# Fixed roles for the PSUM pairs, tanh from gelu's table set, and a new order around the trip's seam

## The reference

```
xn = layernorm(x)
x  = x + mixed_attention(xn) + ternary_ffn(xn)           # layer 0
xn = layernorm(x)
x  = x + hyperbolic_attention(xn) + gated_ffn(xn)        # layer 1

mixed_attention: 16 heads of 8, causal window of 128, plus 4 latent heads over 64 pooled tokens, mixed by a sigmoid gate
hyperbolic_attention: u -> (cosh|u|, sinh|u| u/|u|);  z = max(-<q,k>, 1+1e-7);  scores = -arccosh(z)^2/sqrt(8); causal softmax
gated_ffn: h = silu(x w1 * s1) * (x w2 * s2)              # 128 -> 512
           h = gelu(h h1 * g1);  h = gelu(h h2 * g2);  y = h w3 * s3
```

## Time and profile before

| what | us |
|---|---|
| median of 3 runs | 3143.15 |
| the profiled execution | 3142.96 |
| its span, first to last instruction | 3141.2 |
| PE busy | 2314.6 (74%) |
| PE weight loads, beside PE | 1750.7 (56%) |
| ACT busy | 1760.9 (56%) |
| DVE busy | 1725.3 (55%) |
| POOL busy | 1211.9 (39%) |

### The profile page before, as it was taken

The page is one execution under the profiler, slowest core; times in us unless marked ns, Lnnn a source line. Parts: engine busy times, 40 slices in busy tenths (PEclk is TensorE's granted clock), DMA queues, the critical chain, the costliest instruction groups (busy, mean ns, idle before and its releaser), DMA issues.

```text
span 3141.2 us, 51003 instructions
## 1 busy us (share of the span) xinstructions
PE 2314.6 (74%) x17440; PEld 1750.7 (56%) x17440; DVE 1725.3 (55%) x3470; ACT 1760.9 (56%) x2510; POOL 1211.9 (39%) x1274
## 2 busy tenths in 40 slices
PE   0567877778777778777777787777887777877776
PEld 0345655656555556555565565565665555655555
DVE  7355555655555565655555655565555556555551
ACT  4125655565655555555555565556465556555566
POOL 2224443443443443343343343344244344334332
PEclk9979888989888889988889888898898898988888
DMA  4222212211211211211221221221121121121110
GB/s 127 57 56 56 56 32 55 57 40 47 57 42 42 57 47 40 57 48 37 55 57 30 57 55 30 55 57 41 46 57 42 42 57 46 41 57 49 36 29 4
DMA packets 298755, 153.12 MB, mean 49 GB/s; under 512 B 13360, under 2 KB 295248, under 8 KB 298704
## 3 DMA queue, kind: packets, MB, share of 16 engines
q1 hardware_dynamic: 298704, 152.45, 19.0%
HBM read 81.11 MB, written 71.30 MB: 49 GB/s over the span
## 4 chain that ended last, share of the span: by engine, by line
PE 36%; issue 22%; DVE 19%; ACT 14%; POOL 8%; DMA 0%; DVEq 0%; ACTq 0%; POOLq 0%; SPq 0%
PE pu L1635 6%; PE pu L1454 6%; PE pu L1425 4%; POOL zs L1081 3%; PE pu L1434 3%; DVE nmax L665 3%; DVE zc L829 2%; ACT zc L1274 2%; PE pm L1646 2%; ACT hid L1269 2%; DVE resid L642 2%; PE pu L1468 2%; PE pm L1510 2%; ACT zs L1273 1%; ACT L1269 1%
## 5 line engine op out<-in xcount | busy, mean ns | idle before, releaser
L1425 PE MATMUL pu<-k_st,q_st 128*128 128x128 bf16 (+1 forms) x2048 | 318.4, 265 | 244.6 <-DVE nmax L665 223.6
L1057 POOL TENSOR_SCALAR_AFFINE_SELECT prob<-prob 128x512 f32<-128x512 f32 x128 | 81.5, 637 | 844.1 <-ACT prob L1222 841.9
L1070 POOL TENSOR_TENSOR zs<-zc,zs 128x1024 f32<-128x1024 f32 x160 | 379.8, 2391 | 65.8 <-ACT zc L1274 65.8
L665 DVE TENSOR_REDUCE nmax<-pu 128x4 f32<-128x1024 f32 (+1 forms) x192 | 234.6, 1222 | 307.3 <-PE pu L1434 307.3
L665 DVE TENSOR_REDUCE zmin<-pu 128x4 f32<-128x1024 f32 (+1 forms) x192 | 234.6, 1222 | 268.2 <-PE pu L1434 160.6
L1425 PEld LDWEIGHTS pu<-k_st,q_st 128*128 128x128 bf16 x2048 | 186.5, 106 | 336.7 <-DVE nmax L665 242.3
L1001 POOL TENSOR_TENSOR rs<-ve,mhalf 128x2 f32<-128x2 f32 x64 | 45.7, 714 | 665.1 <-DVE ve L631 658.3
L1635 PE MATMUL pu<-hid,h1t 128*128 128x256 f32 x1024 | 275.2, 417 | 0.0
L1222 ACT ACTIVATE prob<-pu 128x1024 f32<-128x1024 f32 x160 | 163.7, 1024 | 159.3 <-PE pu L1454 159.2
L1635 PE MATMUL pu<-hid,h2t 128*128 128x256 f32 x1024 | 247.2, 385 | 0.0
L829 DVE TENSOR_SCALAR zc<-pu 128x1024 f32<-128x1024 f32 x192 | 232.8, 1212 | 0.0
(11 more groups left out here) (267 smaller groups left out, 5715.7 us busy)
## 6 DMA issues: line engine op xcount, KB each, us to landing
scr<-parts SPq DMA_DIRECT2D x256, 192.0 KB, 2.4
q_st<-scr SPq DMA_DIRECT2D x128, 256.0 KB, 4.1
k_st<-scr SPq DMA_DIRECT2D x64, 512.0 KB, 5.4
scr<-parts SPq DMA_DIRECT2D x128, 128.0 KB, 2.4
x<-in_L_attn_x SPq DMA_DIRECT2D x32, 128.0 KB, 2.1
out<-xold SPq DMA_DIRECT2D x32, 128.0 KB, 1.8
h1t<-in_h1t SPq DMA_DIRECT2D x1, 1024.0 KB, 7.5
h2t<-in_h2t SPq DMA_DIRECT2D x1, 1024.0 KB, 9.8
```

What stands on the lines that cost most here:

```text
L665: return V.tensor_reduce(out=dst, in_=u.ap.rearrange("p (h k) -> p h k", k=width), axis=AX_X, op=op, negate=negate)
L1070: G.tensor_tensor(zs[:, c], zc[:, c], zs[:, c], ALU.add).then_inc(sum_done[1].sem, 1)
L1425: PE.matmul(bank[:, s * width:(s + 1) * width], q_st[layer][:, h // 2, h % 2, q], k_st[layer][:, h // 2, 0:width], start=(s == 0), stop=False)
```

## The change

Five things are done together.

1. **Pairs.** `unit0` holds only min and max units. `av` takes exp0, exp1, exp5, the two attentions, sub0 to sub3, sub5 and f1_0; `unit1` takes exp4, exp2, exp3, f3, sub4, f2 and f1_2.
2. **Silu by tanh.** silu(a) b = (tanh(a/2) + 1) a b / 2. s1 is halved at the start, and s1 s2 is folded into `h1t`, once. ACT computes tanh, in gelu's table set, ahead of the gelus; DVE has two products per half (`gate_values`, `gated`), each over 128x512, in place of two of 128x256.
3. **Embedding** on DVE ahead of the last two min units; PE takes the last min unit behind the last `sub`.
4. **Minima at the seam.** `min0` is the first thing in a trip on PE and DVE.
5. **The order of the rest** on PE, ACT and DVE is written anew: feed3 and feed2 chunks are spread among the square transposes, attention and max units; on ACT one root pair instead of two stands ahead of `operands1`.

The diff, cut to its core; first the pairs, the weights' folding and the products:

```diff
-        UNIT_USES = [uses(M, [EXP[0]]) + uses(L, MIN) + uses(F, MAX) + uses(M, ["f1_0"]),
-                     uses(M, [EXP[4], EXP[2], EXP[5], EXP[3]]) + uses(E, ["f3"] + SUB[1::2]) + uses(L, ["f2"]) + uses(M, ["f1_2"])]
-        AV_USES = uses(M, [EXP[1], "av0", "avT0"]) + uses(E, SUB[0::2] + ["av1", "avT1"])
+        UNIT_USES = [uses(L, MIN) + uses(F, MAX),
+                     uses(M, [EXP[4], EXP[2], EXP[3]]) + uses(E, ["f3", SUB[4]]) + uses(L, ["f2"]) + uses(M, ["f1_2"])]
+        AV_USES = uses(M, [EXP[0], EXP[1], EXP[5], "av0", "avT0"]) + uses(E, SUB[:4] + SUB[5:] + ["av1", "avT1"]) + uses(M, ["f1_0"])
...
+            pre(V.tensor_scalar(s1[:], s1[:], 0.5, None, ALU.mult))
+            pre(V.tensor_tensor(s2[:], s2[:], s1[:], ALU.mult))
+            pre(V.tensor_tensor(h1t[:], h1t[:], bc(s2[:].unsqueeze(2), [P, HC, HID]), ALU.mult))
...
+                a = u.ap.rearrange("p (n k t) -> p n k t", n=2, k=2)[:, :, 0, :]
+                h = hid1[:, chunks[0]:chunks[-1] + 1, :]
+                link(V.scalar_tensor_tensor(h, h, 1.0, a, ALU.add, ALU.mult))
...
+                V.tensor_tensor(h, b, h, ALU.mult).then_inc(u.free, 1)
```

On DVE, in its iteration:

```diff
+                minima(0)
                 if e:
                     spikes(e, link[E])
                     least_squares(e)
-                minima(0)
-                if m:
-                    latent_out(run)
-                minima(1)
                 if f:
                     pool_tokens(run, f, link[F])
+                minima(1)
+                if m:
+                    latent_out(run)
...
                     sinh_series(m, link[M])
-                minima(5)
+                    embedding(m, link[M])
+                minima(4, 5)
...
+                    gate_values(run, m, "f1_0", (0, 1), link[M])
                 if f:
                     shift_lo(run, "mT", 0, f)
                 if m:
-                    gated(run, m, "f1_0", (0, 1))
-                    gated(run, m, "f1_2", (2, 3))
+                    gated(run, "f1_0", (0, 1))
+                    gate_values(run, m, "f1_2", (2, 3), link[M])
+                    gated(run, "f1_2", (2, 3))
```

On ACT:

```diff
                     root(run, l, 0)
-                    root(run, l, 1)
                 if m:
                     operands1(run, m)
                 if l:
+                    root(run, l, 1)
...
+                S.preload_act_table_set(GELU)
+                if m:
+                    tanh(run, m, "f1_0", (0, 1))
                 if f:
                     shift_part(run, "mT", 0)
+                if m:
+                    tanh(run, m, "f1_2", (2, 3))
...
-                    S.preload_act_table_set(SILU)
-                    silu(run, m, "f1_0", (0, 1))
-                    silu(run, m, "f1_2", (2, 3))
```

On PE:

```diff
-                transposes(2)
-                if m:
-                    project1(run)
-                transposes(3)
-                minima(5)
-                transposes(4)
+                feed3(2)
+                if m:
+                    project1(run)
+                feed3(3)
+                transposes(2)
+                minima(4)
+                transposes(3, 4)
...
                 transposes(5)
+                minima(5)
+                feed2(0)
...
                 attend1(0, 1)
+                feed2(1)
                 maxima(1)
                 attend1(2, 3)
-                feed2(0)
+                feed2(2)
                 maxima(2)
-                feed2(1)
+                feed2(3)
                 maxima(3)
```

More of the change, by code:

```diff
@@ L197, in wait_drained @@
         eng.wait_ge(self.free, self.count + 2)
-DVE_LINKS = {"norm": 2, "first": 1, "middle": 27, "last": 1, "end": 6}
+DVE_LINKS = {"norm": 2, "first": 1, "middle": 29, "last": 1, "end": 6}
 def bc(ap, shape):
@@ L841, in least_squares, with gate_values, gated @@
                 V.scalar_tensor_tensor(nmax[1][:], z3, -1.0, z3, ALU.mult, ALU.mult).then_inc(squares_ready.sem, 1)
-            def gated(run, m, name, chunks):
+            def gate_values(run, m, name, chunks, link):
                 u = unit(run, name)
                 dve.wait_ge(sil_ready.sem, sil_ready.at(m, 1 if name == "f1_0" else 2))
[L847 to L850, removed]
+                a = u.ap.rearrange("p (n k t) -> p n k t", n=2, k=2)[:, :, 0, :]
+                h = hid1[:, chunks[0]:chunks[-1] + 1, :]
+                link(V.scalar_tensor_tensor(h, h, 1.0, a, ALU.add, ALU.mult))
+            def gated(run, name, chunks):
+                u = unit(run, name)
+                b = u.ap.rearrange("p (n k t) -> p n k t", n=2, k=2)[:, :, 1, :]
+                h = hid1[:, chunks[0]:chunks[-1] + 1, :]
+                V.tensor_tensor(h, b, h, ALU.mult).then_inc(u.free, 1)
                 if name == "f1_2":
@@ L1248, in operands1, with tanh @@
                 hi_part(1, run.first, m)
-            def silu(run, m, name, chunks):
+            def tanh(run, m, name, chunks):
                 u = unit(run, name)
@@ L1256, in silu @@
                     o = n * BANK
-                    last = S.activation(hid1[:, c, :], u.ap[:, o:o + T], ACT.Silu, scale=s1[:, c:c + 1])
+                    last = S.activation(hid1[:, c, :], u.ap[:, o:o + T], ACT.Tanh, scale=s1[:, c:c + 1])
                 last.then_inc(sil_ready.sem, 1)
@@ L1372, in iteration @@
                 if e:
+                    weights1(run, 2)
+                    hidden(unit(run, "f3"), range(HC), hid3, g2)
                     for n in range(3, UNITS):
@@ L1384, in iteration @@
                 if l:
-                    for n in range(3, UNITS):
-                        root(run, l, n)
+                    root(run, l, 3)
+                    root(run, l, 4)
+                    hidden(unit(run, "f2"), range(HC), hid2, g1)
+                    root(run, l, 5)
                     minima_root(l)
-                    hidden(unit(run, "f2"), range(HC), hid2, g1)
+                if e:
+                    u = misc(run, "yT")
+                    copied(u, out_t[:], u.ap[:, 0:T])
+                S.preload_act_table_set(GELU)
+                if m:
+                    tanh(run, m, "f1_0", (0, 1))
                 if f:
                     shift_part(run, "mT", 0)
+                if m:
+                    tanh(run, m, "f1_2", (2, 3))
                 if e:
@@ L1673, in iteration @@
                 attend1 = lambda *groups: attend(avuse(run, "av1"), 1, groups) if e else None
-                if m:
-                    misc(run.before(), "mT").wait_drained(pe)
-                weights(0, 4, 1)
-                if m:
-                    latent_scores_t(run)
                 if l:
@@ L1682, in iteration @@
                 minima(0)
-                weights(2)
+                if m:
+                    misc(run.before(), "mT").wait_drained(pe)
+                weights(0, 4)
+                if m:
+                    latent_scores_t(run)
+                weights(1, 2)
                 if f:
@@ L1701, in iteration @@
                 attend0(0, 1)
+                if m:
+                    latent_back(run)
                 if f:
@@ L1704, in iteration @@
                 minima(2)
+                attend0(2, 3)
+                if m:
+                    latent_project(run)
                 if e:
@@ L1708, in iteration @@
                 if m:
-                    latent_back(run)
-                attend0(2, 3)
-                if m:
-                    latent_project(run)
-                feed3(1)
-                if m:
                     attended_t(avuse(run, "avT0"), 0)
-                minima(3)
                 if f:
@@ L1719, in iteration @@
                     project_latent(run, f)
-                feed3(2)
                 transposes(0)
@@ L1723, in iteration @@
                     mixed_t(run, m)
-                feed3(3)
+                minima(3)
                 if m:
                     layer0_out(run, m)
-                minima(4)
+                feed3(1)
                 transposes(1)
```

41 lines of the change are left out of this document (16 added, 25 removed).

## The result

The changed kernel takes **2667.59 us** (median of 4 runs, 2661.49 to 2670.63) against 3142.81 for the one before, measured in turn with it: a ratio of **0.8486**, 95% interval 0.847 to 0.8502. The forecast was 2577 with a range of 2464 to 2707, so the sign is as forecast and the gain is 475 us in place of 566. PE is busy for 83% of the span, DVE 69%, ACT 64%, POOL 45%, and the mean granted clock is 0.955.

The account below looks back on a forecast made before the run. PE and its waits bound the kernel: of a 92.5 us trip, 65.3 is full-clock work. With 8.0 of waits the trip becomes 73.3, saving 19.2, 557 over 29 trips plus 9 at the ends: 3143 − 566 = 2577 us, range 2464 to 2707.

Parts of the forecast that it names:

- the ends: Start and partial trips (1, 2, 32, 33): +3 us for folding s1 and s2, −12 for waits, a gain of 9.
- the forecast's own signs: Logarithm every 73 us, no PE wait over 2, clock 0.97 or more, three loads, exp some 8.5 after last max unit.
- the four waits: PE's waits before a max unit (7.3), embedding's transposes (6.1), output projection (2.4), next first scores (1.8): 17.6 us, all to go.
- the 7.3: PE's wait before the third max unit, its reduction queued behind DVE's split; earlier handover and PE fillers would remove it.
- PE's work: PE's work in one trip at full clock: 70.76 − 5.5 = 65.3 us.
- The seam: Between trips: next exp 8.5 us after the last max unit, before 12.6; waits of 2.4 and 1.8 go.
- The table load: ACT's table loads taken at 1.28 us each, without the skill's drain (2.66 in all), which would add 78 us.
- The embedding: Moved 2.5 us earlier in DVE's chain; PE reaches it 0.9 us after it is ready, and the 6.1 wait goes.
- Three priced new waits: New PE waits per trip: yffn 1.5, third square transposes 1.3, split before third max unit 1.05; 3.9 us.
- Rivals 2, 3 and 4: Seam waits for k transfer: 2681, chance 0.15; av pair becomes bound: 3273, 0.04; tanh needs its own load, nothing gained: 0.01.
- the six small ones as today, 4.1: The trip's six other PE waits, longest 1.0, carried over into the new trip's sum at 4.1 us.
- Rival 1: PE's clock keeps falling behind short waits: 5.5 us stay in the trip, +160, 2737 us; chance 0.20.

Follow-up runs that it names:

- e5: Changed kernel with the embedding alone put back behind the last min units on DVE and PE: 2835.89 us.
- e10: As e9, and ACT again takes two root pairs ahead of the handover to the split: 2699.97 us.
- e3: Changed kernel with both edits, that of e1 and that of e2: 2488.29 us.
- e8: e3, and DVE takes the second min unit and the copy of lo ahead of the token sums: 2451.56 us.
- e4: Changed kernel with tanh alone undone: silu from its own table, the old four products, a fourth table load per trip: 2719.21 us.
- e2: Changed kernel with POOL's square of unit 1 moved ahead of its split and that of unit 3 behind the residual: 2571.36 us.
- e1: Changed kernel with the head norm's two-SBUF-operand product (L658) removed, the spike mask entering as a maximum with a PSUM operand: 2574.16 us.
- e7: Changed kernel with fifteen overwritten matmuls added per trip, eight in PE's wait before gr, seven before the last max unit: 2615.87 us.
- e9: Changed kernel with PE's feed2 chunks put back to their old places among the max units: 2683.96 us.

## Why the prediction was right, and where it was short

**Size of the miss.** 91 us on the medians, 93 on the profiled execution: the trips gave 455.6 in place of 557 (101 short), the ends 17 in place of 9. Per trip that is 77.51 against 73.3, of which 0.7 comes from the trip that was read (92.50 where the mean of 29 is 93.22) and 3.5 is the miss. That the ends gave 8 more than forecast is luck: their −12 was not worked out, and no run looked into it. Of the forecast's own signs only the three loads came out in full: trips of 77.5 for 73, a longest wait of 2.07 for 2, a clock of 0.96 and 0.98 for 0.97, the exp at 9.8 for 8.5.

**What held.**
- *The bound and the four waits.* PE and its waits were the right ledger: all four went, and the longest wait that is left is 2.1. The walk's reason for the 7.3 is borne out in part: e5 and e10 show that its early handover and chunks, and the early embedding with the split free of the sums, each keep most of it away.
- *PE's work.* 65.3 at 2.4 GHz; 64.94 and 65.32 in e3 and e8, at clock 1.00.
- *The seam.* Exp at 8.5 forecast, 9.8 measured. The first two tanh ended at 4.5 where 3.05 had been taken, since PE's two projections ahead of them ran in the stretch at clock 0.50. Both waits went all the same.
- *The table load* at 1.28: the load at 1424.03 ends at 1425.31, the logarithm starts at 1425.32. One load more put the exp 1.3 us later in e4. The Trainium skill, "ScalarE: Activation LUTs", What ACT_TABLE_LOAD costs, has 2.66 per switch, by estimate 77 us in 29 trips; neither the rows nor e4 (52 us in all) bear it out here.
- *The embedding.* It ended at 1391.15 (DVE, L812), and its transposes started on PE at 1391.98: 0.8 behind it, 0.9 forecast.
- *Three priced new waits.* yffn 1.2 (lo_t) for 1.5, third sub 1.0 (prob L1323) for 1.3, the split 0 for 1.05: 2.2 in place of 3.9. The split went to the lower bound that was named, the pace of emb's 0.69.
- *Rivals 2, 3 and 4.* The k stack's read was issued at 1408.59; with the 5.4 of the earlier trace rows it is there at 1414.0, and PE's first min unit started at 1421.96, without a wait. PE waits once for ACT before an av unit, 1.0. Three loads per trip.

**What failed** first is one term: "the six small ones as today, 4.1 (some go, others like them come)". They came to 7.3 (9.5 less 2.2), 3.2 more; that the three new waits came to 1.7 less hides half of it. (Of the 1.7 the split gives 1.05: no longer beside the sums, it left no wait.) Small waits were carried over as a constant, though the change moved POOL's squares and sums against DVE's steps; the split's step even said that POOL's sums "come later now", and did not ask what they would then stand beside. They stood beside L658, and the squares beside L747 and L751; gr's wait went from 0.8 to 2.1, local's from 0.4 to 1.3, and nmax has 2.2. That DVE's steps beside POOL's products were the cause is shown by e2, where POOL's work alone moved, by e1, where the step alone went, and by their sum e3, in which waits are 6.2.

The Trainium skill, "SBUF — State Buffer", Who interferes with whom, has the rule: a DVE instruction with two SBUF inputs contends with a GpSimd instruction that reads SBUF, the loser stands for the whole of the other, and one with at most one SBUF input, outside the modes that take both port pairs, does not. The rows agree in all three points (2.06 and 1.55 for steps of 0.19; ends within 0.3 us of the products' ends; 0.19 for L745 and 0.42 for L659, each with one operand in PSUM, beside the first square and the second sum; 0.19 and 0.42 are also what they took in the kernel before, with no product beside them).

**The second part of the miss hangs on the first:** the sum put work at half speed at nothing. Taking the 9.5 for every trip, PE's mean work is 77.51 − 9.5 = 68.0 (67.8 as read over the 29 trips), 2.7 over the 65.3. Rival 1 (the clock keeps falling, 5.5 per trip) was right by half. It is not as that rival had it, short waits at large: in e3 and e8, with ten and eight waits in the trip, the longest 1.2 and 1.0, the clock was 1.00. Here the stretches at 0.59 and 0.50 stand behind the waits of 2.07 and 1.75, and filling these two gave 1.8 per trip back (e7). The row of 1502 to 1519 in the earlier trace rows was the right one to read for short waits. Together: 1.5 more of waits and 2.7 of clock are the 4.2 between 73.3 and 77.51. (Two slips in the prediction's sums change nothing: 2737 + 130 is 2867, and the stand in rival 2 is 2.2.)

**Parts of the gain, as far as they were undone singly:** embedding 168, tanh 52, first minima 16, the feed2 chunks 16, and 32 with the root pairs (e10). The fixed roles of the pairs were not undone by themselves, and parts that share waits need not add up to 475.

## What to carry to other kernels

A reordering moves the overlaps of every pair of engines, not only those it is aimed at: for each long POOL product, list which two-operand SBUF steps of DVE it will now stand beside, above all short ones in a chain that PE waits for. Where they meet, move the POOL work (e2, 96 us), or fold the DVE step into one that reads PSUM (e1, 93 us); in this kernel neither cost anything. And small waits are a term of the sum like others, to be walked one by one and not carried over.

## What the runs showed of the hardware that was not expected

- A DVE step of 0.19 us on 128x32 elements took 2.06 beside a POOL product of 2.32, and 1.55 beside one of 1.87. Steps with one operand in PSUM kept their length beside such products: 0.19 (L745, 128x32) and 0.42 (L659, 128x256).
- The granted clock does not answer to one wait alone. Behind the wait of 2.1 for gr it was 0.59 in one trip of the changed kernel, and in e9 a whole trip with waits of 2.5, 2.1 and 1.5 had 1.00 (65.31 us of work), while over its 29 trips e9 has 0.98 and the changed kernel 0.97. What else decides was not tried.
- Added matrix products made the program faster: 15 more per trip, 1.8 us less (e7).
